# A graph-transformer kernel on one core: half the end rows gathered by POOL, and half of most rounds' gate logits made by DVE

## The reference, cut to what matters

```python
xn = layernorm(x)                                  # 12500 nodes x 256, float32
h = einsum('ni,hif->hnf', xn, W)                   # 8 heads of 32
ea = leaky_relu(s_src[:, src] + s_dst[:, dst])     # 212500 edges, sorted by dst; s_src = h . a_src, s_dst = h . a_dst
ea = exp(ea - segment_max(ea, dst)[dst]);  ea = ea / (segment_sum(ea, dst)[dst] + 1e-8)
gnn = segment_sum(h[src] * ea, dst)
x = x + gnn + mix(xn)                              # linear attention and an MLP of 256-768-256
z = layernorm(x)
logits = z @ gate_w + gate_b                       # 256 x 8: the gates
probs = softmax(logits);  two best experts of 8 per node, each weighted by its probability
x = x + sum over the two of p * (gelu(z @ W1[e] + b1[e]) @ W2[e] + b2[e])     # 256-512-256
```

## Time and profile before

| | |
|---|---|
| median of three executions | 3413.88 us (3394.66 to 3414.95) |
| the execution that was profiled | 3405.85 us |
| its span in the profile | 3403.8 us |
| granted PE clock, mean | 0.912 |
| busy: PE, PEld, DVE, ACT, POOL | 80%, 62%, 59%, 46%, 67% |
| DMA mean over the span | 168 GB/s |

### The profile page before, as it was taken

The page is one execution under the profiler, slowest core; times in us unless marked ns, Lnnn a source line. Parts: engine busy times, 40 slices in busy tenths (PEclk is TensorE's granted clock), DMA queues, the critical chain, the costliest instruction groups (busy, mean ns, idle before and its releaser), DMA issues.

```text
span 3403.8 us, 42546 instructions
## 1 busy us (share of the span) xinstructions
PE 2728.9 (80%) x11623; PEld 2100.2 (62%) x11623; DVE 2024.4 (59%) x5319; ACT 1570.9 (46%) x3411; POOL 2264.1 (67%) x2216
## 2 busy tenths in 40 slices
PE   6817767788888888888888878765279999899997
PEld 5706555566665665656665656543158778778886
DVE  7715556766666766766776666677635646544221
ACT  3405543445455455445455445533145555444442
POOL 0077777777777777777777777772647677666444
PEclk9959988899999999998999999887589999999998
DMA  7797766665665665665665665564756666656553
GB/s 237 245 285 217 201 182 164 166 175 159 171 182 155 173 175 160 170 180 161 172 176 163 166 184 157 153 179 100 272 141 165 145 158 165 144 127 138 101 90 48
DMA packets 403513, 570.77 MB, mean 168 GB/s; under 512 B 73177, under 2 KB 320239, under 8 KB 403098
## 3 DMA queue, kind: packets, MB, share of 16 engines
q0 software_dynamic: 125472, 300.85, 35.2%
q1 hardware_dynamic: 200569, 178.04, 17.9%
q10 hardware_dynamic: 77161, 88.52, 9.7%
HBM read 399.19 MB, written 183.46 MB: 171 GB/s over the span
## 4 chain that ended last, share of the span: by engine, by line
PE 57%; DMA 13%; POOL 9%; ACT 8%; issue 7%; DVE 5%; ACTq 1%; SPq 0%; POOLq 0%; DVEq 0%
PE bank L1196 21%; DMA rows<-table,srcix 10%; PE bank L2077 7%; PE bank L2090 7%; PE bank L1007 6%; POOL rows L1132 5%; PE bank L996 4%; PE bank L969 2%; DMA out<-x_y,x_dest 2%; POOL sorted_d L1619 2%; PE bank L784 2%; PE bank L554 1%; PE bank L555 1%; ACT L1232 1%; PE bank L1178 1%
## 5 line engine op out<-in xcount | busy, mean ns | idle before, releaser
L1132 POOL DMA_INDIRECT rows<-table,srcix x1664 | 1609.6, 967 | 506.9 <-issue 358.9
L1196 PE MATMUL bank<-rows,onehot 128*128 128x272 f32 x3328 | 942.7, 430 | 56.0 <-ACT fout L1246 54.3
L1246 ACT ACTIVATE fout<-bank 128x272 f32<-128x272 f32 x1664 | 639.6, 397 | 558.5 <-PE bank L1196 520.3
L1196 PEld LDWEIGHTS bank<-rows,onehot 128*128 128x128 f32 x3328 | 671.7, 210 | 248.5 <-ACT fout L1246 82.0
L1333 DVE TENSOR_TENSOR rows<-rows,bank 128x1024 f32<-128x1024 f32 x416 | 484.2, 1214 | 210.5 <-ACT rows L1237 210.2
L2162 POOL DMA_INDIRECT out<-x_y,x_dest x210 | 332.5, 1583 | 302.8 <-DMA out<-x_y,x_dest 172.0
L2077 PE MATMUL bank<-x_int,x_w1c 128*128 128x256 f32 x1680 | 394.2, 389 | 18.1 <-issue 10.9
L2090 PE MATMUL bank<-e_w,x_ht 128*128 x1680 | 383.7, 382 | 2.3 <-issue 2.3
L2077 PEld LDWEIGHTS bank<-x_int,x_w1c 128*128 128x128 f32 x1680 | 327.1, 196 | 70.0 <-issue 23.7
L2115 ACT ACTIVATE x_ht<-bank,x_b1c 128x256 f32<-128x256 f32 x420 | 174.2, 470 | 370.4 <-PE bank L2077 370.2
L2090 PEld LDWEIGHTS bank<-e_w,x_ht 128*128 128x128 f32 x1680 | 312.7, 191 | 46.3 <-issue 7.6
(11 more groups left out here) (355 smaller groups left out, 3346.9 us busy)
## 6 DMA issues: line engine op xcount, KB each, us to landing
frag<-fout ACTq DMA_DIRECT2D x104, 544.0 KB
x_in<-sorted_d SPq DMA_DIRECT2D x105, 260.0 KB, 3.4
rows<-table,srcix POOLq DMA_INDIRECT x1664
x_b2c<-in_L_ffn_b SPq DMA_DIRECT2D x105, 128.0 KB, 3.7
frag<-in_x ACTq DMA_DIRECT2D x1, 13416.0 KB
table<-hr SPq DMA_DIRECT2D x24, 544.0 KB, 3.6
xs<-in_x SPq DMA_DIRECT2D x24, 512.0 KB, 6.3
xnt_d<-xt SPq DMA_DIRECT2D x24, 512.0 KB, 5.0
```

The costliest lines, as they stand in the source:

```text
L1132: p.indirect_dma_start(out=B.rows[b][:, j, :], out_offset=None, in_=B.table[:, :], in_offset=bass.IndirectOffsetOnAxis(ap=B.srcix[:, col:c ...
L1196: pe.matmul(B.banks[2 + c % 3][:, 0:ROW], B.onehot[k % 2][:, j, :], B.rows[k % NR][:, j, :], start=True, stop=True).then_inc(S.sum, 1)
L1246: a.activation(B.fout[k % 2][:, j, :], B.banks[2 + c % 3][:, 0:ROW], ACT.Copy).then_inc(S.ev, 1)
```

## The change

**Ends.** POOL gathers only the rows of the chunks' last nodes, 13 gathers in place of 26. The score of a chunk's first node is taken from the chunk before: PE multiplies the scores of the last nodes by the shift matrix (two products into bank 5), and DVE adds `begins`, which is 0 where the chunk starts in the node in which the one before ended, and -BIG where it starts a new one. In `edge_scores` the first column is then the larger of its own value and `sdedge`, where it was a copy. Two small DVE operations in `index_vector` make `begins`.

**Gates.** From the third round on (`FIRST_ROUNDS` is 2) PE and ACT do transposes, copies, gate products and logits for the first super of a round alone. For the second super (10 rounds have one) DVE makes each of 4 tiles x 8 experts = 32 logit columns with one `scalar_tensor_tensor` of 128x256: the product of `e_hn` and the gate weights of one expert, with the sum along the row written to a column of `e_lgd`. The weights are read with a step of 8 words from `e_gw_all`, which holds the 256x8 gate weights in every partition (a new load of 1 MB on SP's queue, behind the loads of the experts' weights). The operations come four at a time, each four 3 steps after the last. Each waits until the one before it is done. One small operation more adds the bias to these columns. `e_lgt` is gone; the logits are copied into `e_hnt`, and in the first two rounds both lie in a free `x_ht`.

```diff
@@ -276,6 +277,7 @@
+        self.begins = A("ends_begins", [P, BLOCKS], F32)
@@ -288,7 +290,7 @@
-        self.ends, self.sd = A("ix_rows", [P, 2 * BLOCKS, ROW], F32), A("ix_sd", [P, 2, BLOCKS, GH], F32)
+        self.ends, self.sd = A("ix_rows", [P, BLOCKS, ROW], F32), A("ix_sd", [P, 2, BLOCKS, GH], F32)
@@ -349,8 +351,9 @@
-        self.e_hn, self.e_hnt, self.e_st = several("e_hn", NH, [P, W, SENT]), A("e_hnt", [P, KD, W * P], F32), several("e_st", 2, [P, W, 16])
-        self.lgt = A("e_lgt", [EXPERTS, W * P], F32)
+        self.e_hn, self.e_hnt, self.e_st = several("e_hn", NH, [P, W, SENT]), A("e_hnt", [P, KD, ST * P], F32), several("e_st", 2, [P, W, 16])
+        self.gw_all, self.gw_x = A("e_gw_all", [P, D, EXPERTS], F32), A("e_gw_x", [P, D], F32)
+        self.lgd = A("e_lgd", [P, ST, EXPERTS], F32)
@@ -431,9 +434,11 @@
     vec(v.scalar_tensor_tensor(out=B.dkey[:, :], in0=B.dprev[:, :], scalar=float(P), in1=B.fl[:, 0, :], op0=ALU.add, op1=ALU.subtract))
+    vec(v.tensor_tensor(B.begins[:, :], B.dprev[:, :], B.fl[:, 0, :], ALU.not_equal))
...
     v.wait_ge(vec.sem, vec.n)
+    vec(v.tensor_scalar(B.begins[:, :], B.begins[:, :], -BIG, None, ALU.mult))
@@ -666,10 +671,10 @@
 def ends_pool(p, S, B):
-    for j in range(2):
-        for b in range(BLOCKS):
-            p.indirect_dma_start(out=B.ends[:, j * BLOCKS + b, :], out_offset=None, in_=B.table[:, :],
-                                 in_offset=bass.IndirectOffsetOnAxis(ap=B.fli[:, j, b:b + 1], axis=0)).then_inc(S.es_in, 16)
+    for b in range(BLOCKS):
+        p.indirect_dma_start(out=B.ends[:, b, :], out_offset=None, in_=B.table[:, :],
+                             in_offset=bass.IndirectOffsetOnAxis(ap=B.fli[:, 1, b:b + 1], axis=0)).then_inc(S.es_in, 16)
@@ -691,12 +696,15 @@
                     ALU.is_equal).then_inc(S.es_sd, 1)
-    v.wait_ge(S.es_in, 16 * 2 * BLOCKS)
-    v.tensor_copy(B.sd[:, :, :, :], B.ends[:, :, D + GH:ROW].rearrange("p (j b) h -> p j b h", j=2)).then_inc(S.es_sd, 1)
+    v.wait_ge(S.es_in, 16 * BLOCKS)
+    v.tensor_copy(B.sd[:, 1, :, :], B.ends[:, :, D + GH:ROW]).then_inc(S.es_sd, 1)
+    v.wait_ge(S.es_tp, 1)
+    v.tensor_tensor(B.sd[:, 0, :, :], B.banks[5][:, 0:BLOCKS * GH].rearrange("p (b h) -> p b h", h=GH),
+                    B.begins[:, :].unsqueeze(2).to_broadcast([P, BLOCKS, GH]), ALU.add).then_inc(S.es_sd, 1)
     for q in range(PARTS // 2):
-        v.wait_ge(S.es_tp, q + 1)
+        v.wait_ge(S.es_tp, q + 2)
         v.tensor_copy(parts[:, 2 * q * ENDS:2 * (q + 1) * ENDS], B.banks[1 + q][0:CB, 0:2 * ENDS]).then_inc(S.es_sd, 1)
-    v.wait_ge(S.es_tp, PARTS // 2 + 1)
+    v.wait_ge(S.es_tp, PARTS // 2 + 2)
@@ -704,12 +712,16 @@
     pe.wait_ge(S.es_sd, 2)
+    lasts = B.sd[:, 1, :, :].rearrange("p b h -> p (b h)")
+    pe.matmul(B.banks[5][:, 0:BLOCKS * GH], B.shift[:, 0:P], lasts, start=True, stop=False)
+    pe.matmul(B.banks[5][:, GH:BLOCKS * GH], B.shift[:, P:2 * P], lasts[:, 0:(BLOCKS - 1) * GH], start=False, stop=True).then_inc(S.es_tp, 1)
+    pe.wait_ge(S.es_sd, 3)
...
             t.then_inc(S.es_tp, 1)
-    pe.wait_ge(S.es_sd, 2 + PARTS // 2)
+    pe.wait_ge(S.es_sd, 3 + PARTS // 2)
@@ -1305,7 +1317,7 @@
         v.wait_ge(vec.sem, vec.n)
-        vec(v.tensor_copy(sdm[:, 0:1], B.sdedge[:, 0, k:k + 1]))
+        vec(v.tensor_tensor(sdm[:, 0:1], sdm[:, 0:1], B.sdedge[:, 0, k:k + 1], ALU.max))
@@ -1559,20 +1571,36 @@
 GATES = 2 * P // EXPERTS
+GATES_AT, GATES_GAP = NORM + 4 - MOMENTS - MOMENT_STEPS, 3
...
     return BOTH + LAG + 1 + n + 6
+def by_tensor(r):
+
+    return ROUNDS[r] if r < FIRST_ROUNDS else ROUNDS[r][:1]
+
+def supers_to(r):
+    return sum(len(by_tensor(q)) for q in range(r))
 def turns_to(r):
-    return 3 * sum(len(q) for q in ROUNDS[:r])
+    return 3 * supers_to(r)
 def gates_to(r):
-    return sum(len(q) + 1 for q in ROUNDS[:r])
+    return supers_to(r) + r
+
+def turned(B, r, kk):
+
+    return B.ht[kk][:, :, :].rearrange("p k n -> p (k n)") if r < FIRST_ROUNDS else B.e_hnt[:, kk, :]
@@ -1670,6 +1698,8 @@
                 sp.dma_start(B.w2[:, e * HT:(e + 1) * HT, :], B.a["L0_ffn_W2"][e].rearrange("(k p) n -> p k n", p=P)).then_inc(S.x_w, 16)
+            sp.dma_start(B.gw_all[:, :, :].rearrange("p d e -> p (d e)"),
+                         B.a["L0_ffn_gate_w"].rearrange("d e -> (d e)").partition_broadcast(P)).then_inc(S.e_wd, 16)
@@ -1688,9 +1718,9 @@
     def steps(r):
-        n = R_TILES[r]
+        n, mine = R_TILES[r], by_tensor(r)
         yield from idle(TURN)
-        for q, k in enumerate(ROUNDS[r]):
+        for q, k in enumerate(mine):
@@ -1700,22 +1730,22 @@
             yield from idle(TURN_GAP)
-        yield from idle(GATE - TURN - TURN_GAP * len(ROUNDS[r]))
+        yield from idle(GATE - TURN - TURN_GAP * len(mine))
         pe.wait_ge(S.e_w, 32)
-        pe.wait_ge(S.e_t, turns_to(r) + 2 * len(ROUNDS[r]))
-        for i, k in enumerate(ROUNDS[r]):
+        pe.wait_ge(S.e_t, turns_to(r) + 2 * len(mine))
+        for i, k in enumerate(mine):
...
             for kk in range(KD):
-                t = pe.matmul(bk[i][0:EXPERTS, 0:m * P], B.gw[:, kk, :], B.e_hnt[:, kk, o * P:(o + m) * P], start=(kk == 0), stop=(kk == KD - 1))
+                t = pe.matmul(bk[i][0:EXPERTS, 0:m * P], B.gw[:, kk, :], turned(B, r, kk)[:, o * P:(o + m) * P], start=(kk == 0), stop=(kk == KD - 1))
...
         pe.wait_ge(S.e_carry, r)
-        for i in range(n):
-            t = pe.transpose(bk[3][:, (GATES + i) * EXPERTS:(GATES + i + 1) * EXPERTS], B.lgt[:, i * P:(i + 1) * P],
+        for i in range(sum(SUPERS[k][1] for k in mine)):
+            t = pe.transpose(bk[3][:, (GATES + i) * EXPERTS:(GATES + i + 1) * EXPERTS], turned(B, r, 0)[0:EXPERTS, i * P:(i + 1) * P],
@@ -1734,7 +1764,7 @@
     def steps(r):
-        x, hn, st = B.e_x[r % NF], B.e_hn[r % NH], B.e_st[r % 2]
+        x, hn, st, theirs = B.e_x[r % NF], B.e_hn[r % NH], B.e_st[r % 2], by_tensor(r)
@@ -1756,19 +1786,19 @@
         a.wait_ge(S.e_gate, gates_to(r))
-        for i, k in enumerate(ROUNDS[r]):
+        for i, k in enumerate(theirs):
...
             for kk in range(KD):
-                a.wait_ge(S.e_tp, 2 * (2 * r + i) + kk + 1)
-                a.activation(B.e_hnt[:, kk, o * P:(o + m) * P], bk_columns(B, kk, m), ACT.Copy).then_inc(S.e_t, 1)
+                a.wait_ge(S.e_tp, 2 * (supers_to(r) + i) + kk + 1)
+                a.activation(turned(B, r, kk)[:, o * P:(o + m) * P], bk_columns(B, kk, m), ACT.Copy).then_inc(S.e_t, 1)
             yield from idle(TURN_GAP)
-        yield from idle(GATE + 1 - TURN - TURN_GAP * len(ROUNDS[r]))
-        for i, k in enumerate(ROUNDS[r]):
+        yield from idle(GATE + 1 - TURN - TURN_GAP * len(theirs))
+        for i, k in enumerate(theirs):
...
             a.wait_ge(S.e_gate, gates_to(r) + i + 1)
-            a.activation(B.lgt[:, o * P:(o + m) * P], B.banks[i][0:EXPERTS, 0:m * P], ACT.Copy).then_inc(S.e_t, 1)
+            a.activation(turned(B, r, 0)[0:EXPERTS, o * P:(o + m) * P], B.banks[i][0:EXPERTS, 0:m * P], ACT.Copy).then_inc(S.e_t, 1)
@@ -1824,6 +1854,20 @@
                                op1=ALU.mult).then_inc(S.e_mom, 1)
+    def gates(r):
+
+        v.wait_ge(S.e_wd, 16)
+        for k in ROUNDS[r][1:]:
+            s, m = SUPERS[k]
+            for i in range(m):
+                for half in range(2):
+                    v.wait_ge(S.e_hn, s + i + 1)
+                    for e in range(half * EXPERTS // 2, (half + 1) * EXPERTS // 2):
+                        v.wait_ge(vec.sem, vec.n)
+                        vec(v.scalar_tensor_tensor(out=B.gw_x[:, :], in0=B.e_hn[r % NH][:, s - R_FIRST[r] + i, 0:D], scalar=1.0,
+                                                   in1=B.gw_all[:, :, e], op0=ALU.mult, op1=ALU.mult, accum_out=B.lgd[:, i, e:e + 1]))
+                    yield from idle(GATES_GAP)
@@ -1835,6 +1879,11 @@
                 waits -= MOMENTS + MOMENT_STEPS
+            if len(by_tensor(r)) < len(ROUNDS[r]):
+                own = sum(SUPERS[k][1] for k in ROUNDS[r][1:])
+                yield from idle(GATES_AT)
+                yield from gates(r)
+                waits -= GATES_AT + 2 * own * GATES_GAP
@@ -1844,9 +1893,16 @@
         v.wait_ge(S.e_w, 32)
-        v.tensor_tensor(L, bk[3][:, GATES * EXPERTS:(GATES + n) * EXPERTS].rearrange("p (t e) -> p t e", t=n), over_tiles(B.gb[:, :]), ALU.add).then_inc(S.e_got, 1)
+        of_pe = sum(SUPERS[k][1] for k in by_tensor(r))
+        bias = lambda m: B.gb[:, :].unsqueeze(1).to_broadcast([P, m, EXPERTS])
+        if of_pe < n:
+            v.wait_ge(vec.sem, vec.n)
+            vec(v.tensor_tensor(B.lg[:, of_pe:n, :], B.lgd[:, 0:n - of_pe, :], bias(n - of_pe), ALU.add))
+        v.tensor_tensor(B.lg[:, 0:of_pe, :], bk[3][:, GATES * EXPERTS:(GATES + of_pe) * EXPERTS].rearrange("p (t e) -> p t e", t=of_pe),
+                        bias(of_pe), ALU.add).then_inc(S.e_got, 1)
...
         v.wait_ge(S.e_got, r + 1)
+        v.wait_ge(vec.sem, vec.n)
```

1 line of the change is left out of this document (added).

## The result

The changed kernel takes 3420.69 us (median of 20 runs, 3411.47 to 3425.87) against 3410.24 us for the one before (20 runs): a ratio of 1.0026, with a 95% interval of 1.0016 to 1.0035, so 5 to 12 us slower. Measured a second time, beside e5 to e7, it was 1.0019 (1.0008 to 1.0030), 3 to 10 us slower. The forecast was 3400 us, 5 us less than the profiled execution before. The time lies in the range and within 1% of the forecast, but the sign is wrong. The nearness says little: the whole sum was worth 5 us of 3400.

The account below looks back on a forecast made before the run. The prediction took POOL as the bound, in the edge stage and, with PE right behind, in routing and experts. From 3405.85 us, -16.3 + 0.4 - 6 + 4.5 + 12 = -5.4 gave 3400 us, range 3360 to 3452.

Parts of the forecast that it names:

- Ends, -16.3 us: Edge stage: 13 end gathers fewer, 1.25 us apart, save 16.3 us if POOL is still never idle.
- The rival of gathers that only queue: Edge stage: rows asked for 16 us earlier land no earlier, the 16.3 not gained: 3416 us; chance 0.09.
- PE's relief, -6: Routing: PE loses 31.7 us of work; a third of POOL's 17.2 us of waits for DVE returns, bounds 0 and -17.
- The reading that POOL bounds the stage: Routing and experts: POOL sets the end, with PE right behind.
- The operation, 0.66 us: Routing: one gate operation on DVE takes 0.66 us, bounds 0.47 and 0.86; 32 are 21.1 us a round.
- DVE's room, 0 (0 to +10): Routing: 22.0 us of DVE's waits a round hold 21.1 us of work; buffers and queueing slots absorb lateness.
- The slower rival: Routing: DVE becomes the bound, deciding from 0.69 us an operation; 3454 us at 0.86 us; chance 0.19.
- The third round, +4.5 (0 to +9): First round with gates: the 32 operations stand ahead of an `x_y`, so POOL's store comes 3 to 9 us later.
- Meeting of DVE and POOL, +12 (0 to +30): Gates' stretches: two-input DVE operations hold POOL's instructions 0.19 us on average, 16 a round; 30 us if nothing absorbs it.
- The sum: Whole kernel: ends -16.3, `index_vector` operations +0.4, PE's relief -6, third round +4.5, DVE and POOL meeting +12: -5.4 us.

Follow-up runs that it names:

- e5: Changed kernel with gate weights turned once by ACT, so the gate operations read adjacent words: 3397.60 us, 0.9948 of the kernel before.
- e7: Changed kernel with copies in place of gate operations in the third and fourth round (other logits): 3403.20 us, 0.9970 of the kernel before.
- e1: Kernel before with the ends' part of the change alone, routing as before: 3391.18 us, 0.9940 of the kernel before.
- e4: Changed kernel with each round's 32 gate operations replaced by four copies of 8 words: 3387.54 us, 0.9927 of the kernel before.
- e6: Kernel before with the gate operations added on DVE, result unused, PE doing all its work: 3434.45 us, 1.0060 of the kernel before.
- e2: Kernel before with the gates' part of the change alone: 3431.72 us, 1.0059 of the kernel before.
- e3: Changed kernel with gate operations reading one SBUF input and one value per partition (other logits): 3401.98 us, 0.9975 of the kernel before.
- e12: Repeat of e4 on a chip with slower gathers: 0.9905 of the kernel before, which took 3849.25 us there.

## Why the prediction was wrong

**Ends, -16.3 us.** Right: the last stage starts 17.0 us earlier in e1 and 10.5 and 12.3 in the two profiles of the changed kernel, within a scatter of the edge stage that is that wide. The rival of gathers that only queue is out: e1 has the whole gain. `sdedge` came at 212.62 (212.8 worked out) and the first scores at 218.74 (218.9).

**PE's relief, -6.** Too much. e4 shows 2 us, e6 against e2 none. The step took a third of POOL's five waits for DVE's results, 17.2 us, as PE's doing. Four of the five, 11.4 us, were no waits for DVE. This is one of them, and the end of the result that it stored, in the timeline before:

```profile
2764.04 0.69 DVE L2147 TENSOR_TENSOR x_y<-x_y,x_scale 128x512 f32<-128x512 f32 x1
...
2783.31 1.54 POOL L2162 DMA_INDIRECT out<-x_y,x_dest  x1 [4.33 <-DVE x_y L2147]
```

The profile names DVE, but the result had been done for 18.6 us; in the other three for 16 to 26. What came last, 0.85 to 1.03 us ahead of the store, was the landing of the slot before's stores. The fifth is the third slot's, 5.82 us, the only one that a quicker result could have shortened. The reading that POOL bounds the stage was right, and stronger than the prediction took it.

**The operation, 0.66 us.** Right: 0.68, and 32 of them 22 us a round.

**DVE's room, 0 (0 to +10).** This is the step that failed. It compared 22.0 us of waits in a round with 21.1 us of work, and let six output buffers and the slots that queue at POOL take up the lateness in between. For the later rounds that holds: from the sixth slot on POOL never waited for a result of DVE's on the quick chips, and e3, with more of DVE's time, needs less there than any other kernel. At the start it does not. The prediction let a result wait behind up to 20 operations, 13 us. The order of the fourth round, shown ahead of it, has 28 between two slots' results, 19 us, with only three small rows among them. And the store in front of POOL is not yet built up there: POOL still waited 8.80 us for DVE three slots earlier, and at the fifth slot 4.5 us of lateness could be taken up, where 13.3 came. The waits of DVE for POOL's buffers, from which the prediction read that slots were queueing, are sums over nine rounds. An average room was applied to the one place where it is not there. The slower rival put the limit at 0.69 us an operation for all rounds; the loss lay at the start, at 0.68.

In the changed kernel the 7.5 us of the fourth round are not made up behind it. From the sixth slot on every result lay ready, so POOL's own chain sets the time, and e7, which has no operations in the two first rounds, is 11 to 15 us earlier than the changed kernel at the 5th slot and 14 to 17 at the end. On the other chips, where POOL waits for DVE again and again, the fourth round alone left nothing that the medians show.

**The third round, +4.5 (0 to +9).** About right: 5 to 9 us at the first store, 1 to 5 by the 4th slot against before, 4 to 7 against e4.

**Meeting of DVE and POOL, +12 (0 to +30).** Right in mechanism and near in size. POOL's busy time in the last stage is 641.4 to 645.2 us in the five profiles with the changed kernel's operation, 625.4 to 631.8 in before, e1, e3 and e4: 10 to 20 us more. The last stage of e7 is 9.7 us longer than e4's, for eight rounds of it. In e5, with operations of 426 ns, the busy time is 632.6 us, hardly more than without any. How much is taken up, the working left open: for eight rounds it had 24 us if nothing is, and 8 to 10 were left.

**The sum.** -16.3 + 0.4 - 6 + 4.5 + 12 was -5.4. With what the profiles show, 2 us for the relief (e4), 14 to 17 for the third and the fourth round together (e7 against the changed kernel) in place of 4.5 + 0, and 10 for the later rounds (e7 against e4), it would have been +6 to +9, against +5 to +12 measured. The largest error is the start's, 10 to 13 us; the relief's 4 go the same way.

## What to carry to other kernels

Idle time of an engine summed over rounds is room only where the engine behind it has finished work in store. Before work is laid into such gaps, look in the order for the longest run of it between two results that someone waits for, and multiply. At the first place where it occurs, compare that with the time between the two results before, and with how long the second one lay finished until it was taken. What is over is lost, and it stays lost when another engine bounds the rest. Where a profile says that an engine waited for a result, look up when that result was done: an older one was not what ended the wait. And shorten the operation before moving it: two thirds of the length took the price in the last stage from 22 us to 1.

## What the runs showed of the hardware

A multiplication with a sum along 256 words took 426 ns with adjacent words and 625 ns with one input that steps by 8 words: (625 - 426) / 256 = 0.78 ns more a word. The nearest rows of before had given 0.71 (1.75 against 1.04 ns). The written sum is an instruction of its own of 83 ns that starts before the multiplication's end; an operation and the wait for it take 0.68 us together. `tensor_scalar` with the stepping words as its one SBUF input beside a value per partition is longer, not shorter: 677 ns for 256 words, 628 for 230.

The operation with two SBUF inputs holds an indirect store of POOL's that starts into it, 1.98 us against 1.54; with one SBUF input the stores' mean is 1588 ns, against 1633. The mean alone is a weak sign: without any gate operation it is 1583 ns in before and 1612 in e1.

The Trainium skill (Vector Engine (DVE) Microarchitecture Reference, §7) says that this kind of operation runs at half rate with two SBUF sources that aren't bf16. e5's 426 ns for 256 float32 words, 1.04 ns a word as in the earlier trace rows, disagrees, and the measurement decides. Of the two figures of its §5.2 that the prediction used, 1.73 ns a column is for one source that hops each element, 2.50 for both sources or the output alone by 24 words. The change has one stepping source, and the first is near: with the 161 ns at no words of the earlier trace rows, (625 - 161) / 256 = 1.81 ns.

The kernel before took 3411 to 3414 us on two chips and 3849 to 3889 on two others. Most of it lies in the edge stage: the last stage of e4 began at 2364 us, that of e12, the same kernel, at 2732. It then took 1026 us in the one and 1087 in the other. So two kernels were compared only on one chip, and the last stage's length only on the quick ones.
